# An attention pipeline whose five engines run through each step in another order

## The reference

```python
def _L0_xattn_ref(query, key, value, mask, Wq, bq, Wk, bk, Wv, bv, Wo, bo):
    ...                                     # 16 heads of 8 numbers
    q = proj(query, Wq, bq)
    k = proj(key, Wk, bk)
    v = proj(value, Wv, bv)
    q = _rope(q)
    k = _rope(k)
    scores = jnp.einsum('bhqd,bhkd->bhqk', q, k) / math.sqrt(hd)
    ...
    p_attn = jax.nn.softmax(scores, axis=-1)
    x = jnp.einsum('bhqk,bhkd->bhqd', p_attn, v)
    ...
    return x @ Wo.T + bo
...
x = x + jnp.tanh(g_xattn[0]) * _L0_xattn_ref(_layernorm(x, axis=-1), ctx_1024, ctx_1024, ...)
x = x + jnp.tanh(g_ffn[0]) * _L0_ffn_ref(_layernorm(x, axis=-1), ...)   # argmax of 8 experts, GELU
```

## Time and profile before

| | us |
|---|---|
| median of 3 runs | 294.68 (293.27 to 297.7) |
| profiled execution | 294.33, span 292.5 |
| attention steps, from the maxima of tile 3 to those of tile 29 | 140.84 in 26 steps |
| PE, DVE, ACT, POOL busy | 237.4, 188.7, 165.9, 178.2 |

### The profile page before, as it was taken

The page is one execution under the profiler, slowest core; times in us unless marked ns, Lnnn a source line. Parts: engine busy times, 40 slices in busy tenths (PEclk is TensorE's granted clock), DMA queues, the critical chain, the costliest instruction groups (busy, mean ns, idle before and its releaser), DMA issues.

```text
span 292.5 us, 13366 instructions
## 1 busy us (share of the span) xinstructions
PE 237.4 (81%) x5065; PEld 201.2 (69%) x5065; DVE 188.7 (64%) x638; ACT 165.9 (57%) x482; POOL 178.2 (61%) x221
## 2 busy tenths in 40 slices
PE   1257899888798898879888896788789899999960
PEld 1146777677676676757666675577679899999950
DVE  1636758788789669798888957775576444444420
ACT  1235758788667668567878675335364344444420
POOL 2275745756647859748898686711877755555550
PEclk9999979999799989799999999758999999999995
DMA  7899000303030401204000000132132533111100
GB/s 229 244 380 358 14 2 10 106 13 103 3 112 12 119 16 56 90 2 131 16 12 25 13 26 12 37 89 55 53 116 79 147 108 100 55 30 32 38 20 0
DMA packets 23729, 22.41 MB, mean 77 GB/s; under 512 B 3792, under 2 KB 19173, under 8 KB 23668
## 3 DMA queue, kind: packets, MB, share of 16 engines
q1 hardware_dynamic: 20388, 15.75, 17.6%
q0 software_dynamic: 2272, 4.46, 4.6%
q10 hardware_dynamic: 1008, 1.35, 1.4%
HBM read 16.50 MB, written 5.51 MB: 75 GB/s over the span
## 4 chain that ended last, share of the span: by engine, by line
PE 56%; DVE 19%; issue 11%; POOL 5%; ACT 3%; DMA 2%; SPq 0%; POOLq 0%; DVEq 0%; ACTq 0%
PE ps L734 12%; PE ps L788 10%; DVE mx L1227 8%; PE ps L778 5%; PE ps L745 5%; PE ps L764 5%; PE ps L763 3%; PE ps L717 3%; PE ps L715 3%; PE ps L716 3%; PE ps L810 2%; DMA x_all<-in_x 2%; PE ps L855 2%; PE ps L703 1%; POOL rows L501 1%
## 5 line engine op out<-in xcount | busy, mean ns | idle before, releaser
L549 POOL DMA_INDIRECT out<-fin,got x39 | 37.9, 972 | 27.5 <-DVE fin L1286 22.0
L1227 DVE TENSOR_REDUCE mx<-ps 128x16 f16<-128x1024 f32 x32 | 39.1, 1222 | 18.6 <-PE ps L745 18.1
L501 POOL DMA_INDIRECT rows<-x_all,dest_i x32 | 32.8, 1025 | 19.5 <-DVE x_all L1062 12.3
L734 PE MATMUL ps<-w_f,hT 128*128 x312 | 44.5, 286 | 0.0
L788 PE MATMUL ps<-vx,pr 128*64 128x32 f32 x1024 | 39.5, 234 | 2.8 <-DVE on L1162 2.4
L788 PEld LDWEIGHTS ps<-vx,pr 128*64 128x64 f32 x1024 | 36.0, 150 | 7.1 <-ACT pr L578 2.4
L734 PEld LDWEIGHTS ps<-w_f,hT 128*128 128x128 f32 x312 | 37.8, 191 | 1.0 <-issue 0.3
L528 POOL TENSOR_TENSOR rot<-qk,cf 128x256 f32<-128x256 f32 x32 | 23.4, 730 | 24.7 <-ACT qk L600 17.4
L515 POOL TENSOR_TENSOR stk<-rot,stk 128x256 f16<-128x256 f32 x32 | 21.7, 678 | 25.1 <-DVE stk L1240 25.0
L1286 DVE SCALAR_TENSOR_TENSOR fin<-ps,got 128x128 f32<-128x128 f32 x39 | 13.7, 350 | 36.0 <-PE ps L734 34.9
L578 ACT ACTIVATE pr<-ps 128x1024 f32<-128x1024 f32 x32 | 32.7, 1021 | 6.7 <-PE ps L832 6.7
(11 more groups left out here) (156 smaller groups left out, 615.4 us busy)
## 6 DMA issues: line engine op xcount, KB each, us to landing
got<-rows SPq DMA_DIRECT2D x39, 72.0 KB, 1.9
w_f<-in_W_rows SPq DMA_DIRECT2D x8, 256.0 KB, 3.1
w_r<-in_W_last_row SPq DMA_DIRECT2D x8, 256.0 KB, 4.3
w_f<-in_L_ffn_W SPq DMA_DIRECT2D x8, 256.0 KB, 4.7
x_all<-in_x SPq DMA_DIRECT2D x3, 512.0 KB, 8.3
xt_all<-in_x_t SPq DMA_DIRECT2D x3, 512.0 KB, 7.2
ct_all<-in_ctx SPq DMA_DIRECT2D x3, 512.0 KB, 7.5
out<-fin,got POOLq DMA_INDIRECT x39, 2.3
```

The source lines that it names most:

```text
L501: pool.indirect_dma_start(out=rows, out_offset=bass.IndirectOffsetOnAxis(ap=dest_i[:, t:t + 1], axis=0), in_=x_all[:, t, :], in_offset=Non ...
L549: pool.indirect_dma_start(out=out_d, out_offset=bass.IndirectOffsetOnAxis(ap=got_i[:, u % GOT, R_ID:R_ID + 1], axis=0), in_=fin[:, u % FRI ...
L734: mm = pe.matmul(o, hT[:, par, c, :], w2_f[:, bass.ds(e, 1), c, :].rearrange("p o n -> p (o n)"), start=False, stop=(c == FC - 1))
L1227: dve.tensor_reduce(mx[:, t % 2, :].rearrange("p (w r) -> p w r", w=4)[:, :, 0:NA], ps_s[:, :].rearrange("p (w a k) -> p w a k", w=4, k=S) ...
```

## The change

No operation is added or removed. Each engine's order within a step is another one, and two buffers differ.

- DVE: x2 of tile i-6 (and the routing's place, where there is one) moves ahead of q scaling; the maxima of tile i-2 move behind the two casts of tile i.
- PE: the maxima are transposed in the next step, behind the projections (tile i-3), then the normalised output, then PV, and only then the stack; the second half of the scores moves behind the transposed scores.
- ACT: the copy of the output's transpose moves ahead of the k copy, the router part behind it, the values ahead of `kT` and `qT`.
- POOL: the scatter moves behind the rotation.
- The values get five buffers in place of four, and the maxima's transpose moves to bank 7, with waits of PV and of the maxima's transpose that keep the two apart.

```diff
+VRING = 5
-        vx = sb("vx", [P, RING, 2, 8, 32])
+        vx = sb("vx", [P, VRING, 2, 8, 32])
-        ps_mx = bank[5].bitcast(F16)[:, 0:P]
+        ps_mx = bank[7].bitcast(F16)[:, 4 * P:5 * P]
...
@@ gpsimd
-                for _ in range(SCATTER_AT.get(i, 0)):
-                    scatter()
                 t = i
                 if live(t):
                     par = t % 2
...
                     pool.tensor_tensor(rot[:, par, :], rot[:, par, :], rot_s[:, par, :], ALU.add).then_inc(rope_done, 1)
+                for _ in range(SCATTER_AT.get(i, 0)):
+                    scatter()
...
@@ scalar
+                t = i - 5
+                if live(t):
+                    act.wait_ge(onT_done, t + 1)
+                    wait(act, op_done, t - 1)
+                    act.activation(onT[:, t % 2, :], ps_onT, ACT.Copy).then_inc(onT_ev, 1)
...
-                    act.activation(x_all[:, t, R_LOGIT:R_LOGIT + NE], ps_lx, ACT.Copy).then_inc(lx_ev, 1)
...
                     act.activation(qk[:, par, D:2 * D], ps_kv[:, 0:D], ACT.Identity, scale=mask_s[:, t:t + 1]).then_inc(k_ev, 1)
+                    act.activation(x_all[:, t, R_LOGIT:R_LOGIT + NE], ps_lx, ACT.Copy).then_inc(lx_ev, 1)
...
@@ tensor
+                t = i - 3
+                if live(t):
+                    pe.wait_ge(mx_done, t + 1)
+                    wait(pe, on_done, min(T, i - 4))
+                    wait(pe, mxT_ev, t)
+                    pe.transpose(ps_mx, mx[:, t % 2, :], ident_h).then_inc(mxT_done, 1)
...
+                t = i - 5
+                if live(t):
+                    if t == 0:
+                        pe.wait_ge(s_cs, 2)
+                    pe.wait_ge(on_done, t + 1)
+                    wait(pe, x2_done, t)
...
+                    pe.transpose(ps_onT, on[:, t % 2, :], ident).then_inc(onT_done, 1)
+                t = i - 4
+                if live(t):
+                    s, par = t % VRING, t % 2
+                    pe.wait_ge(p_rdy, t + 1)
+                    pe.wait_ge(v_ev, t * 4 + 4)
+                    wait(pe, on_done, t)
+                    pe.wait_ge(mxT_ev, min(T, t + 2))
...
@@ vector
+                t = i - 6
+                if live(t):
+                    dve.wait_ge(op_done, t + 1)
+                    dve.wait_ge(lx_ev, t + 1)
+                    dve.tensor_tensor(x_all[:, t, 0:QX], ps_op, x_all[:, t, 0:QX], ALU.add).then_inc(x2_done, 1)
+                if third is not None:
+                    route_place(third)
                 t = i
                 if live(t):
                     if t == 0:
...
-                t = i - 2
-                if live(t):
-                    dve.wait_ge(s_done, t + 1)
-                    wait(dve, mxT_done, t - 1)
-                    dve.tensor_reduce(mx[:, t % 2, :].rearrange("p (w r) -> p w r", w=4)[:, :, 0:NA],
...
                     dve.tensor_copy(win[:, H:2 * H, :].rearrange("p h (c d) -> p h c d", c=4)[:, :, 1:4:2, :], k_f
                                     ).then_inc(hi_done, 1)
+                t = i - 2
+                if live(t):
+                    dve.wait_ge(s_done, t + 1)
+                    wait(dve, mxT_done, t - 1)
+                    dve.tensor_reduce(mx[:, t % 2, :].rearrange("p (w r) -> p w r", w=4)[:, :, 0:NA],
```

More of the change, by code:

```diff
@@ L608, in step @@
                     act.activation(tg[:, :], gates[:, :], ACT.Tanh).then_inc(s_tg, 1)
+                t = i
+                if live(t):
+                    s = t % VRING
+                    wait(act, pv_done, t - VRING + 1)
+                    if t == 0:
+                        act.wait_ge(s_v1, 2)
+                    v_ps = ps_kv[:, D:2 * D].rearrange("p (j hh d) -> p j hh d", hh=2, d=HD)
+                    for b in range(2):
+                        for hh in range(2):
+                            act.activation(vx[64 * hh:64 * hh + 64, s, b, :, 16 * hh:16 * hh + HD],
+                                           v_ps[64 * b:64 * b + 64, :, hh, :], ACT.Copy).then_inc(v_ev, 1)
                 t = i - 1
@@ L616, in step @@
                                    ).then_inc(qT_ev, 1)
-                t = i
-                if live(t):
[L619 to L632, removed]
                 if i - 2 in EXPERT_AT:
@@ L765, in step @@
                     pe.matmul(ps_kv[:, 0:D], pick, bk_h[:, :], start=False, stop=True).then_inc(qkv_done, 1)
+                t = i - 3
[4 more added lines that the diff above has]
+                    pe.transpose(ps_mx, mx[:, t % 2, :], ident_h).then_inc(mxT_done, 1)
+                if i == 3:
+                    pe.wait_ge(s_vo, 64)
+                    pe.matmul(bank[4][:, 0:NE], wo_n[:, :], id_wr[:, P:QX], start=True, stop=True).then_inc(s_wox, 1)
+                t = i - 5
+                if live(t):
+                    if t == 0:
+                        pe.wait_ge(s_cs, 2)
+                    pe.wait_ge(on_done, t + 1)
+                    wait(pe, x2_done, t)
+                    if i - 3 in GROUP_AT:
+                        pe.wait_ge(g_read, GROUP_AT[i - 3] + 1)
+                    pe.transpose(ps_onT, on[:, t % 2, :], ident).then_inc(onT_done, 1)
[6 more added lines that the diff above has]
+                    pe.wait_ge(mxT_ev, min(T, t + 2))
+                    for j in range(8):
+                        for b in range(2):
+                            mm = pe.matmul(ps_o[S * b:S * b + S, 32 * j:32 * j + 32], pr[:, par, NA * (j % 2) + j // 2, b, :],
+                                           vx[:, s, b, j, :],
+                                           start=True, stop=True)
+                    mm.then_inc(pv_done, 1)
                 t = i - 1
@@ L779, in step @@
                     mm.then_inc(stk_done, 1)
[L780 to L791, removed]
                 if tile(i - F0):
@@ L834, in step @@
                     mm.then_inc(st_done, 1)
+                t = i - 2
+                if live(t):
+                    pe.wait_ge(half_done, t + 1)
+                    scores(t, 1).then_inc(s_done, 1)
                 if i - 2 in GROUP_AT:
@@ L849, in step @@
                     second_layer(i - F0 - 2)
[L850 to L855, removed]
                 if i == 4:
@@ L1182, in step @@
                                              in1=w1_h[:, e, :], op0=ALU.mult, op1=ALU.subtract).then_inc(s_w1lo, 1)
-                t = i - 6
-                if live(t):
-                    dve.wait_ge(op_done, t + 1)
-                    dve.wait_ge(lx_ev, t + 1)
-                    dve.tensor_tensor(x_all[:, t, 0:QX], ps_op, x_all[:, t, 0:QX], ALU.add).then_inc(x2_done, 1)
-                if third is not None:
-                    route_place(third)
                 t = i - 6
@@ L1241, in step @@
                                     ).then_inc(hi_done, 1)
+                t = i - 2
+                if live(t):
+                    dve.wait_ge(s_done, t + 1)
+                    wait(dve, mxT_done, t - 1)
+                    dve.tensor_reduce(mx[:, t % 2, :].rearrange("p (w r) -> p w r", w=4)[:, :, 0:NA],
+                                      ps_s[:, :].rearrange("p (w a k) -> p w a k", w=4, k=S), AX.X, ALU.max
+                                      ).then_inc(mx_done, 1)
                 if i == 3:
```

6 lines of the change are left out of this document (1 added, 5 removed).

## The result

The changed kernel takes 318.74 us (median of 4, 317.0 to 321.17) against 295.19 us (293.27 to 297.7) on the same chip: 1.083 times as long, 95% interval 1.072 to 1.094. Forecast were 308.6 us and a range up to 318: the direction was right, the size 10 us too small. The profiled execution took 319.44 us (span 317.7), 25.1 more than the 294.33 of before.

What follows compares the result with a forecast made beforehand. Bound: a 4.94 us circle of maxima, casts, low halves, stack transposes, PV and scores, which covers the rotation. Profiled 294.33 + 11.6 for the stage + 2.7 for the last attention steps = 308.6 us; range 301 to 318 us.

Steps and rivals of the forecast that it cites:

- The closed chain: Regular step: q scaling, k copy, rotation, casts and maxima become one chain returning to itself on DVE, 5.66 us a step.
- the maxima's transposes in bank 7: Buffer move on PE, costed at nothing together with the sooner values, copied halves last and five value buffers.
- PE's own way: PE's round from maxima over output transpose, PV and scores to the next maxima: 5.23 us, 0.43 short of binding.
- Scatter, values, low halves at nothing: POOL's moved scatter and low halves and ACT's sooner value copies stay off the chain; gain and cost nothing.
- Irregular DVE work: Routing, statistics and weight splitting between q scaling and casts fit the 3.4 us the chain leaves DVE free; routing steps become free.
- The rule on casts beside POOL's work: Rival: second cast on DVE blocked by POOL's scatter, up to 0.8 us in 16 steps, +13, 321 us; chance 0.08.
- DVE's end blocks: Blocks ending DVE's step in steps 8, 20 and 30 now lie between maxima and reciprocal, in the chain: 3.91 us.
- After tile 29: Last five attention steps, without rotation: the wait for x2 still stands ahead of PV; 0 to 2.75 us, taken as 2.7.
- PE's inner stalls: Pauses among PE's score matmuls come again; 0.43 us hidden, 0.7 left, two of over 1 us: 1.4 us.
- The falling clock: Rival: PE idles more, the granted clock falls to 0.50 in half the steps, +9 us, 318 us; chance 0.12.
- The forecast's 152.5 us for the stage: From tile 3's maxima to tile 29's: 26 x 5.66 = 147.2, with 3.9 and 1.4, against 140.84 before.

Runs made afterwards that it cites:

- Experiment 3: Changed kernel with ACT's copy of the transposed output put back behind the k copy and the logits' copy; 313.64 us, ratio 1.062 to the kernel before.
- 2: Kernel before with only DVE's maxima moved behind the two casts; 326.40 us, ratio 1.102.
- 1: Changed kernel with DVE's maxima put back ahead of the two casts, the rest as changed; 320.89 us, ratio 1.086 to the kernel before.
- 6: Changed kernel with POOL's scatter put back ahead of the rotation; 318.69 us, ratio 1.084 to the kernel before.
- 10: Kernel before with ACT's order alone changed to values (five buffers), kT, onT, qT; 296.02 us, ratio 0.997.
- experiment 5: Changed kernel with 48 tiny extra matmuls on PE ahead of its first matmul; 330.95 us, ratio 1.122 to the kernel before.
- experiment 4: Changed kernel with two extra matmuls per step in PE's idle time ahead of the maxima's transpose; 316.45 us, ratio 1.072 to the kernel before.
- 8: Kernel before with both halves of the scores on PE moved directly behind the projections, ahead of stack transposes and PV; 296.21 us, ratio 0.994.
- 9: Kernel before with PE's scores ahead of the stack transposes and ACT's order values (five buffers), kT, onT, qT; 290.14 us, ratio 0.981.

## Why the prediction was right and where it was wrong

- **The closed chain: right.** 5.73 us a step against 5.66; 26 steps make 1.8 us of the miss. The link that is longer is the output transpose behind the maxima's transpose (0.43 instead of 0.35), so "the maxima's transposes in bank 7", costed at nothing, were not quite free. Experiment 3 shows that the chain passes through the onT and k copies, 2 that the maxima behind the casts close it, 1 that PE's own way (put at 5.23; the scores were over 5.0 after the maxima) is the next bound.
- **Scatter, values, low halves at nothing: right but for one step.** The totals of experiments 6 and 10 show no price, and the stack transposes, which in regular steps of before started 0.07 us behind the low halves, now start 0.23 us or more behind them; but behind the rotation the scatter cost 0.86 us in the routing step.
- **Irregular DVE work: wrong in one step.** "So the routing steps that cost today become free" reckoned with the durations of before; L976 took 1.64 us instead of 0.18 beside POOL's work, and the step lost 1.0. Why it was held up there and not in experiment 6 is not shown.
- **The rule on casts beside POOL's work: no rival after all.** Casts beside a scatter took 0.28 to 0.36 us, but once 0.53, where the routing work of L976 had already made the casts late; in the timeline of the changed kernel:

```profile
127.08 1.06 POOL L502 DMA_INDIRECT rows<-x_all,dest_i  x1 [0.17 <-issue]
...
127.46 0.31 DVE L1233 CAST stk<-rot 128x256 f16<-128x256 f32 x1
127.70 0.53 DVE L1234 CAST stk<-rot 128x256 f16<-128x256 f32 x1
```

The Trainium skill, "SBUF — State Buffer", section "Who interferes with whom", would have the later one blocked to the end; the trace shows that at most for this one cast, which ended 0.09 us behind the scatter. The work that POOL did hold up was L976, which the prediction had not looked at.
- **DVE's end blocks: right in kind.** 3.0 us instead of 3.91.
- **After tile 29: right in number, the reason not shown.** 2.9 us instead of 2.7, but behind tile 29's maxima the clock was at 0.50 for 21.6 us, against 13.7 before, so the agreement may be luck.
- **PE's inner stalls: wrong, the term was mis-sized.** "There are two of over 1 us: 1.4" took the pauses to come again as they had been. They cost 4.4, because they are tied to the crossing of a block in PE's stream and not to a place of the work: nine of them fell into seven steps of the stage, and experiment 5 moved them by moving the stream.
- **The falling clock: wrong to leave it out of the sum.** It stood as a rival, at 9 us with a chance of 0.12. The seven of 26 steps in which it was seen lost 5.1 us. The row at 0.50 behind a pause was in the kernel before already, and a step with more idle time on PE was forecast; experiment 4 shows that filling this idle time holds the clock. So the two belonged together and into the sum at some part of the 9.

The forecast's 152.5 us for the stage is short by 10.2: regular steps 1.8, pauses 3.0, clock 5.1, the routing step 1.0 and rests 0.3, less 0.9 for the end blocks. The chain made 308.6 and the irregular steps the rest, which put the time just past the range's end.

Open is whether the new order of PE brings more pauses than the old one (nine, and four, six and four in experiments 1, 3 and 6, with the new; three, and one and five in experiments 2 and 10, with the old; none in experiments 8 and 9, with the scores ahead of the stack transposes), and why the clock was down for 17 us at a stretch, from 122.0 on, in experiment 9, whose PE was busy for 85% of the span against 75% in the changed kernel.

## What to carry to other kernels

An engine that takes its instructions in order joins chains: before moving one behind another, add up the round that closes through it and compare it with the next longest round, for a change of order pays the longer of the two (4.95, 5.51, 5.73 and 6.03 us came from the same work). A move that frees one engine hands the wait to the engine whose copies come later for it, and only the pair of moves gains (experiments 8, 10 and 9). Price pauses and a lower clock in the sum, at the slack that the new round leaves, not as a rival beside it.

## What the runs showed of the hardware

PE paused 0.5 to 1.5 us at nine of 28 boundaries of 256 of its instructions, eight of them in or right behind dense small matmuls, and went on 2.2 to 2.9 us after the load of the next block had begun. A small operation of DVE (L976) once took 1.64 us instead of 0.18 beside POOL's low halves and rotation. Two projection-sized matmuls a step in PE's idle time kept the granted clock at 1.00 for 153.6 us, where the same kernel without them fell to 0.50 (1.2 GHz) six times, first at 62.15, after PE had stood idle for 2.05 us up to 61.37; PV of 1.12 us took 1.87 there.
